# The loop-closing branches of all engine programs carry a branch hint

## The reference

```
xn = layernorm(x);  x = x + L0_attn(xn) + L0_ffn(xn)   # fast-weight attention; router with low-rank experts
xn = layernorm(x);  x = x + L1_attn(xn) + L1_ffn(xn)   # ALiBi softmax attention, 16 heads; mixture of 8 experts
xn = layernorm(x);  x = x + L2_attn(xn) + L2_ffn(xn)   # forgetting attention forward and backward, 16 heads;
                                                       # two layers of local attention and gated feed-forward
xn = layernorm(x);  x = x + L3_attn(xn) + L3_ffn(xn)   # feature-map attention; mixture of 8 SwiGLU experts
```

## Time and profile before

| | |
|---|---|
| median of three runs | 4214.52 us |
| the profiled execution's own time | 4224.95 us |
| its span on the chip | 4222.8 us |
| TensorE matmuls busy | 3817.7 us (90% of the span) |
| VectorE busy | 2775.5 us (66%) |
| ScalarE busy | 1878.4 us (44%) |
| GpSimd busy | 645.2 us (15%) |
| mean granted TensorE clock | 0.94 of full speed |

### The profile page before, as it was taken

How to read it: one execution, slowest core, us unless ns; L and a number is a source line. 1 busy time by engine, 2 the same in 40 slices (tenths; PEclk the granted TensorE clock), 3 DMA queues, 4 the chain that set the end, 5 groups by cost and what they waited for, 6 DMA issues and landing times. The chain is left out here.

```text
span 4222.8 us, 86111 instructions
## 1 busy us (share of the span) xinstructions
PE 3817.7 (90%) x30766; PEld 2993.4 (71%) x30766; DVE 2775.5 (66%) x7915; ACT 1878.4 (44%) x3484; POOL 645.2 (15%) x736
## 2 busy tenths in 40 slices
PE   3677999999998999999999999999978998998988
PEld 3565777777775676666666666666657887888877
DVE  2554555555554666666666666666647888888888
ACT  0001222222222455555555555555545555555555
POOL 0000000000000122212211222222212222222222
PEclk8668999999998999999999999999989999999999
DMA  5000000000000000000000000000001000000000
GB/s 131 10 7 23 0 0 0 0 0 0 0 0 36 5 9 10 9 9 9 9 9 9 9 9 9 9 9 9 9 5 47 1 2 2 1 2 2 1 2 3
DMA packets 29333, 44.63 MB, mean 11 GB/s; under 512 B 5928, under 2 KB 20816, under 8 KB 28368
## 3 DMA queue, kind: packets, MB, share of 16 engines
q1 hardware_dynamic: 29136, 41.56, 3.9%
HBM read 24.38 MB, written 4.19 MB: 7 GB/s over the span
## 5 line engine op out<-in xcount | busy, mean ns | idle before, releaser
L242 PE MATMUL bank<-l_kT,l_qT 32*128 32x128 f32 (+1 forms) x3072 | 407.4, 360 | 1.1
L1600 ACT ACTIVATE l_probsT<-bank 128x768 f32<-128x768 f32 x256 | 207.6, 811 | 443.3 <-PE bank L242 442.5
L142 POOL TENSOR_TENSOR l_rstd<-l_var,w_neg_half 128x2 f32<-128x2 f32 (+1 forms) x92 | 67.4, 733 | 2044.0 <-DVE l_var L137 2044.0
L242 PE MATMUL bank<-l_qm,l_kT 32*128 32x128 f32 (+1 forms) x3072 | 371.2, 335 | 0.0
L1573 POOL TENSOR_TENSOR l_rinv<-l_ssm,w_neg_half 128x8 f32<-128x8 f32 x128 | 210.2, 1642 | 731.7 <-DVE l_ssm L1841 731.6
L261 DVE TENSOR_REDUCE l_negmax<-bank 128x2 f32<-128x256 f32 (+1 forms) x384 | 197.5, 514 | 185.6 <-PE bank L242 180.5
L242 PEld LDWEIGHTS bank<-l_kT,l_qT 32*128 32x128 f32 x3072 | 227.9, 192 | 88.5 <-issue 80.8
L859 ACT ACTIVATE l_probsT<-bank 128x768 f32<-128x768 f32 x128 | 103.4, 808 | 411.4 <-PE bank L242 411.4
L230 PE MATMUL bank<-masks,ident 128*128 128x256 bf16 x1536 | 248.9, 281 | 40.8 <-issue 32.3
L2021 PE MATMUL bank<-l_xnT,w_egate 128*128 128x256 f32 x1024 | 276.4, 394 | 0.0
L2021 PE MATMUL bank<-l_xnT,w_eup 128*128 128x256 f32 x1024 | 270.1, 387 | 0.0
(11 more groups left out here) (308 smaller groups left out, 8567.1 us busy)
## 6 DMA issues: line engine op xcount, KB each, us to landing
l_v_half<-l_v SPq DMA_DIRECT2D x32, 264.0 KB, 3.2
l_v_half<-l_v SPq DMA_DIRECT2D x32, 132.0 KB, 3.1
x_all<-in_x SPq DMA_DIRECT2D x16, 128.0 KB
w_up<-in_up SPq DMA_DIRECT2D x1, 2048.0 KB
w_down<-in_down SPq DMA_DIRECT2D x1, 2048.0 KB
scratch<-l_y SPq DMA_DIRECT2D x128, 16.0 KB
w_egate<-in_egate SPq DMA_DIRECT2D x1, 2048.0 KB, 8.4
out_x<-x_all SPq DMA_DIRECT2D x16, 128.0 KB, 1.8
```

The source lines that it names most:

```text
L242: lasts.append(pe.matmul(bank[:, at:at + n * P], lhs[:, c * P:(c + 1) * P], rhs[:, x0 * P:(x0 + n) * P], start=False, stop=(i == 1), skip_ ...
L1600: Bt.took(act.activation(probsT[:, (j // 2) % 2, 2 * (j % 2):2 * (j % 2) + 2, :], two[:, :, 0:AW], ACT.Exp), rd, use)
```

## The change

```diff
+def looped(nc, eng, start, end):
+
+    return nc.Fori(start, end, engines=[eng.engine], hint_back_edge=True)
...
-            with sp.Fori(0, rounds) as rd:
+            with looped(nc, sp, 0, rounds) as rd:
...
-            with pe.Fori(0, rounds // 2) as pair:
+            with looped(nc, pe, 0, rounds // 2) as pair:
...
-            with pe.Fori(0, B) as it:
+            with looped(nc, pe, 0, B) as it:
...
-            with eng.Fori(2, B) as it:
+            with looped(nc, eng, 2, B) as it:
```

More of the change, by code:

```diff
@@ L463, in _ @@
             g.wait_layer(pool, 0)
-            with pool.Fori(0, rounds + 1) as rd:
+            with looped(nc, pool, 0, rounds + 1) as rd:
                 pool.wait_ge(var_ready, rd + 1)
@@ L469, in _ @@
         def _(act):
-            with act.Fori(0, rounds + 1) as rd:
+            with looped(nc, act, 0, rounds + 1) as rd:
                 G.wait_taken(act, rd, A_LOGIT)
@@ L587, in _ @@
                     first[x]()
-            with dve.Fori(0, rounds // 2) as pair:
+            with looped(nc, dve, 0, rounds // 2) as pair:
                 for h in range(2):
@@ L835, in _ @@
             g.wait_layer(pool, 0)
-            with pool.Fori(0, B + 1) as n:
+            with looped(nc, pool, 0, B + 1) as n:
                 pool.wait_ge(var_ready, n + 1)
@@ L854, in _ @@
             queries(0)
-            with act.Fori(0, B) as it:
+            with looped(nc, act, 0, B) as it:
                 def probabilities(u):
@@ L927, in _ @@
                 part(0)
-            with dve.Fori(0, B) as it:
+            with looped(nc, dve, 0, B) as it:
                 ch = Chain(dve, dve_chain, it, n_chain)
@@ L2056, in _ @@
             norm_rstd(pool, g, st, NC).then_inc(rstd_ready, 1)
-            with pool.Fori(0, B) as it:
+            with looped(nc, pool, 0, B) as it:
                 ch = Chain(pool, pool_chain, it, FB)
@@ L2114, in _ @@
             g.issue_late_loads(sp)
-            with sp.Fori(0, B) as it:
+            with looped(nc, sp, 0, B) as it:
                 sp.wait_ge(x_done, it + 1)
```

## The result

The changed kernel takes 4171.72 us (median of 7 runs, 4168.05 to 4197.30) against 4214.52 us in 7 runs of the kernel before on the same chip. The ratio is 0.9916, with a 95% interval of 0.9897 to 0.9935, so it is 27 to 43 us faster by this interval. The medians differ by 42.8 us, at the edge of it, because three of the seven runs took 4184.62 to 4197.30 us. The forecast was 4138 us. The sign was right, and the gain is about half of the forecast one. The profiled execution took 4171.72 us itself; its span is 53.0 us shorter than that of the earlier trace rows.

The account below looks back on a forecast made before the run. TensorE, busy 90% of the span, was taken as the bound, stalling at layer 2's branch back. Terms -86.4 + 2 + 2 + 3 = -79.4 us, taken as -77 unprofiled: 4214.5 to 4138 us, range 4120 to 4188.

Parts of the forecast that it names:

- what a pass costs: Layer 2 loop on TensorE: a pass at full clock costs 105.65 us plus its gap; 13 passes without gaps 1373.4 us.
- the full effect: Layer 2 loop on TensorE: all gaps (32.3 us) and half clock (54.1 us) go, -86.4 us; chance 74%.
- the target's code is brought before the branch: TensorE's branch back in layer 2: falls to 0.21 us, hidden by 2.1 us of queued work; 0.15 us left per pass.
- a fetch in 10 us leaves room for one more ahead of the branch: Layer 2 fetch queue: 142 fetches in 1460 us, longest stall 4.8 us, so the target's fetch fits before the branch.
- The other argument: Layer 2: some nine other fetches come per pass and none makes TensorE wait; its longest other waits are 0.4 us each.
- The count: Instruction fetches in layer 2's loop: should stay about 11 a pass, since the body is as long as before.
- A: Layer 2 branch only partly hidden, fetch too late or second block missing: gaps of 1.5 to 2.3 us stay, 4176 us; 12%.
- B: The hint does nothing for TensorE's layer 2 branch; gaps and clock falls stay, added instructions cost 2 us: 4216 us; 8%.
- C: Loops whose bodies fit, above all TensorE's in layers 1 and 3: hint fetches code already held, up to 4335 us; 6%.
- The added instruction: Hint instruction on every engine: 60 ns per pass, bare on VectorE in layer 1 (0.9 us), +2 us in all.
- The exits: Loop ends: code after the last pass may be fetched late because fetches follow the hint; +3 us.
- the gaps went and the clock still fell: Sign against the forecast, behind TensorE's layer 2 edges: idle time then didn't cause the half clock (54.1 us).

## Why the prediction was wrong, and what in it was right

**Right: what a pass costs.** A pass at full clock is 105.65 us plus its gap. In the changed kernel 107.28 - 1.63 = 105.65 and, at the edge of 2270.50 us, 106.66 - 0.99 = 105.67 us; with the branch at slot 64, 105.64. Where the whole stall is gone a pass takes 105.49 us, and the loop 1374.56 us where the forecast had 1373.4. So the price of the full effect, 86 us in layer 2, was right, and a placed loop head gets it (1459.83 - 1374.56 = 85.3 us). Nothing else was late next.

**Wrong: "I expect that the target's code is brought before the branch."** This step failed, and I took 2 us left where 15.5 us of gaps and 12.0 us of half clock were left. The hint is honoured, but only from about the start of the block in which the branch lies, so here the target's fetch started 0.1 to 1.0 us after the branch and the branch took 2.50 to 3.65 us where I had 0.21. The argument I used, a fetch in 10 us leaves room for one more ahead of the branch, spoke of the room in the queue. It did not speak of when the fetch starts. The other argument had a misreading besides: TensorE's longest wait beside the gaps was 0.6 us (line 1419, above) and not 0.4. The trace of before could have warned me: two fetches stand at an edge there, the first of them 0.1 to 0.8 us after the branch, so a block starts near the branch. I had counted the fetches of a pass, and not looked at where they stand. The count was off too: I had expected it to stay at 11 a pass, and it fell to 10, and to 9 with the branch at slot 188, since a needless one is saved.

**The rivals.** A was the one that happened, in its mechanism ("the fetch starts too late"). I gave it 12%. That its time (4176 us) is so near is in part luck: it had 43 us of gaps and half clock left in layer 2, and 27.5 were. Of these 15.5 us some 10 don't show in the medians, since the profiled execution of before lay 10.4 us above its median and that of the changed kernel is the median run. B is ruled out by the kernel with the hint in that one loop (0.9905, 0.988 to 0.993). C is ruled out by the kernel with all other hints (1.0012, 0.9994 to 1.003) and by layer 1's passes, with no fetch and 882.9 us against 882.8.

**The small terms.** The added instruction takes 39 to 40 ns on TensorE and VectorE in layer 2, where I had 60, and cost nothing in layer 1, where I had it bare at 0.9 us. The exits, where I had 3 us, cost nothing behind TensorE's loop of layer 2 (the 23.98 us above), and 1.5 or 1.6 us in the two kernels with the branch at slot 250. The 2.4 us behind layer 2 and 1.8 us ahead of layer 1's loop can't be told from the spread of executions, since all but this one hint together are worth 1.0012 (0.9994 to 1.003). The 1.7 us in layer 3 are likelier to be the hints' own: its 15 passes took 971.6 to 972.3 us in the five profiles without hints there, and 972.3 to 974.2 in the eight with them.

**The clock.** The forecast said that I'd be wrong if the gaps went and the clock still fell. The gaps shrank and the clock fell twice. In the kernel before the falls sorted neatly by the length of the gap (none at 2.28 us and below). That sorting was chance, for it didn't hold elsewhere. Without hints at slot 188 the clock fell after 1.44 us and not after 2.00; without hints at slot 32 it fell after 2.22 us and not after 2.75:

```profile
1622.70:1736.41 113.71, 110.18 (x1039) 78.47 (x1038) 73.69 (x211) 63.05 (x116) 23.57 (x19) 0.94 0.04 9
...
2070.67:2179.07 108.40, 104.14 (x1039) 74.39 (x1038) 73.42 (x211) 63.06 (x116) 23.57 (x19) 1.00 0.04 9
```

What decides between two gaps of a like length is open. That gaps bring the long falls as such is borne out: with no gap, or at most 0.8 us, at the edges (slots 188, 250 and 64 with hints) no pass had more than 3.4 us of half clock, and at 0.8 to 1.3 us (slot 32 with hints) neither. Slot 171 had falls of 10 to 14 us after gaps of 1.0 us, which lie seven matmuls into the pass, so a short gap isn't always safe.

## What to carry to other kernels

If a loop body doesn't fit on its engine, hint its way back and also put its loop head so that the branch lies well into its fetch block (64 slots sufficed here, 32 did not) and so that the target's block holds more than a few instructions; the hint alone gave about half of what both gave. The other 18 hints together brought nothing that could be measured (1.0012, 0.9994 to 1.003). Look at the gap and at the clock behind it: here the half clock cost more than the wait.

## What the runs showed of the hardware

- The branch hint is an instruction of 31 to 50 ns on TensorE. Given over 100 us ahead of the branch, it isn't acted on then: the target's fetch starts some 5.6 us ahead of the branch at slots 188 and 250, 3.4 us at 171, 0.7 at 64, and 0.1 us or more behind its start at 32 and 8.
- At a taken branch to code that isn't there, the branch takes 4.0 to 4.8 us with two fetches at it, 3.3 to 3.9 with one that starts about 1 us or more after it, 2.5 to 3.1 if it starts within 0.8 us of the branch's start, 1.6 to 2.1 from slot 64 (once 2.6), and 0.34 to 0.38 us when the target was fetched 3 us before or earlier. Queued matmuls hide part of it at this place: the gap is 1.7 to 1.9 us shorter than the branch.
- The placement of a loop moves the time even without a hint: 0.9968 (0.995 to 0.9986) for the whole kernel at slot 188, nothing at slot 32.
- With no gaps left, TensorE's clock still had single stretches of 3.4 us at half speed, two or three in the 13 passes of slots 188 and 250 (1.6 us of time each: 107.11 against 105.49), and none at slot 64. Slot 32, with gaps, had four. What brings them stays open.
